# Delta-rule attention and a top-2 expert layer on one core: a new order of the first tile's loads and small vector work, and expert numbers of the first two expert tiles read once

## Chip, cores, metric

One core of one Trainium2 chip. The time is device microseconds of one launch; the kernel before took 901.56 us, the median of 3 runs (900.86 to 904.77). All start times below are microseconds from the start of the profiled span.

## What is computed

The reference, cut to what matters (x is 8 x 512 x 256 in fp32; 4 heads with keys of 128 and values of 64; 8 experts with a hidden width of 1024):

```python
x = x + attn(layernorm(x))          # delta rule
#  q, k, v, g = x@Wq, x@Wk, x@Wv, x@Wg ; beta = sigmoid(x@Wb)
#  k = k * rsqrt(sum(k*k) + 1e-12) ; q = q * DK**-0.5
#  per token: S += k (beta (v - k.S))^T ; o = q.S
#  o = o * rsqrt(mean(o*o) + eps) * norm_w * silu(g) ; return o @ Wo
x = x + ffn(layernorm(x))
#  probs = softmax(x @ router.T) ; the best 2 of 8 experts per token
#  out = sum over the 2 of prob * (gelu(x @ w1[e].T) @ w2[e].T)
```

## The kernel before, in words

Everything is written by hand, one instruction stream per engine, with a named semaphore for each hand-over. An engine executes its stream in order, so the order of the Python calls is the schedule.

**Attention.** The 4096 tokens are T = 32 tiles of 128. Each engine has a loop over i in which it calls stages of several tiles at once (`gram(i - 2)`, `k_proj(i - 1)` and so on): a software pipeline that is fixed in the program text. Tile n goes through: `ln1_stats` (DVE, line 1716: BN_STATS, BN_AGGR, add eps), `ln1_scale` (POOL, line 622: a power -0.5 at line 620, then a product at line 630), `ln1` (ACT, xn), `xnT_make` (PE transposes, line 1203), `xnT_evac` and `xnT_low` (fp16 high part by ACT, low part by DVE, line 1732), `k_proj`, `beta_proj`, `q_proj` (PE), `k_square` and `beta_exp` (ACT), `k_norm` (DVE, lines 1761 and 1763: the argument karg), `kscale_` (POOL: karg to the power -0.5 in line 620), `k_prime` (DVE, line 1772: k' = k times kscale), `k_transposes` (PE, line 1262), `kT_evac` (ACT) and `kT_low` (DVE, line 1747), `gram` (PE), `masked_l` (DVE, line 1792, nL), and then the inversion of a triangular matrix in 7 levels, the state update and the output. All products run as three fp16 products of high and low parts, so each weight is split too: `weight_hi(n)` on ACT, then `weight_lo(n)` on DVE (line 1906; n = 1 is wq, 2 is wvg, 3 is wo) and `wk_lo` (line 2082).

**Before the loops** stand the prologues. SP issues the loads (x tile 0, the small constants of `fc`, the identity `ident`, wb, wq, ...). POOL's prologue is `ln1_scale(0)`, one line on rowA that waits for `fc`, and `ln1_scale(1)`; its loop then begins with `kscale_(0)`. The change doesn't touch POOL's stream.

**Experts.** After the attention, tokens are gathered by expert into tiles of 256 tokens. `up(i, q, ms)` makes the hidden layer of expert tile 4i+q, 8 groups m of 6 matmuls with 256 columns; `down(i, q, ms)` makes the output from 8 groups m of 4 matmuls (columns 512, 256, 512, 256). Which expert a tile has is a number in SBUF (`tile_table`) that PE's sequencer reads into a register (`expert_of`, line 1558: TENSOR_LOAD), since the number is an address of the weights. `up` and `down` read it anew on each call. Between the parts of the first expert tiles stand the last steps of attention tile T-1: `xn2T_make`, `logits_make`, `rank` and others. ACT applies gelu (`hidden`), DVE makes the low part (`hidden_lo`, line 2266) and then the routing of the last group (`best_logit` to `expert_masks`, which writes `both`), and PE's `rank` (8 small matmuls) needs `both`.

```python
def parts_of(i, q):
    ...
    return [(expert_of(i, q), slice(0, PE_TOK))]

def ln1_scale(n):
    ...
    done(pool, s_mv, n)
```

Of the kernel before, what the change touches and what calls it, by code (L numbers as in the profile page):

```python
# [4 lines left out]
P = 128  # L5
# [3 lines left out]
T = B * N // P  # L9
# [3 lines left out]
KH = HID // P  # L13
EPS = 1e-5
PE_TOK = 2 * P
# [56 lines left out]
def build(nc, x, wq, wk, wvg, wb, wo, norm_w, router, w1, w2, eye, fconst, iconst, out):  # L72
# [3 lines left out]
    with ctx:  # L76
# [16 lines left out]
        wq_s, wk_s = wqk[:, 0, :, :, :], wqk[:, 1, :, :, :]  # L93
# [366 lines left out]
        def _(sp):  # L460
# [40 lines left out]
            load_x(0)  # L501
            sp.dma_start(fc[:, 3 * P:FCONST], fconst[:, 3 * P:FCONST]).then_inc(s_fc, 16)
            sp.dma_start(ident, fconst[:, 0:P]).then_inc(s_ident, 16)
# [288 lines left out]
        def _(act):  # L792
# [173 lines left out]
            def weight_hi(n, dst, src, scale=A_SCALE):  # L966
                act.wait_ge(s_wload[n], 16)
                evac(dst, src, scale).then_inc(s_wsh, 1)
# [30 lines left out]
            weight_hi(2, wvg_s[:, 0, :, :], wvg_in)  # L999
            k_square(0)  # L1000
            beta_exp(0)
            q_evac(0)
# [144 lines left out]
            xn2T_evac(T - 1)  # L1147
            logits_copy(T - 1)
            hidden(0, 0, range(3, 4))
# [19 lines left out]
        def _(pe):  # L1169
# [405 lines left out]
            def up(i, q, ms=range(KH)):  # L1575
                owners = parts_of(i, q)
# [47 lines left out]
            up(0, 0, range(0, 2))  # L1624
# [4 lines left out]
            up(0, 0, range(2, 4))  # L1629
# [3 lines left out]
            up(0, 0, range(4, 6))  # L1633
            wo_make(T - 1)
            done(pe, s_z, T - 1)
            up(0, 0, range(6, 8))
            up(0, 1, range(0, 2))
            xn2T_make(T - 1)
            up(0, 1, range(2, 4))
            logits_make(T - 1)  # L1640

            up(0, 1, range(4, 6))
            xT_make(0, 2)
            up(0, 1, range(6, 8))
            done(pe, s_lg, T - 1)
            rank(T - 1, p_rank_last, p_tot_last)
# [3 lines left out]
            down(0, 0)  # L1650
# [49 lines left out]
        def _(dve):  # L1700
# [371 lines left out]
            def next_stats(n):  # L2072
                if n > 1:
                    ln1_stats(n)
# [14 lines left out]
            dve.scalar_tensor_tensor(wb_s[:, 1, :, :], wb_in[:, :, :], A_SCALE, wb_s[:, 0, :, :], ALU.mult, ALU.subtract).then_inc(s_wbl, 1)  # L2089
            ln1_stats(1)  # L2090
            dve.wait_ge(s_fc, 16)
# [4 lines left out]
            weight_lo(1, wq_s, wq_in).then_inc(s_wsl, 1)  # L2096
            weight_lo(2, wvg_s, wvg_in).then_inc(s_wsl, 1)
            k_norm(0)
# [10 lines left out]
            q_low(0)  # L2109
            k_prime(0)  # L2110
            dve.wait_ge(s_normw, 1)
            weight_lo(3, wo_s, wo_in, normw_s[:, 0:1]).then_inc(s_wsl, 1)
# [89 lines left out]
            for i in range(T + 3):  # L2202
# [40 lines left out]
                kT_low(i - 3)  # L2243
# [121 lines left out]
            hidden_lo(0, 0, range(0, 3))  # L2365
# [13 lines left out]
            hidden_lo(0, 0, range(3, 4))  # L2379
# [99 lines left out]
```

## Time and profile before

| what | value |
|---|---|
| median of 3 runs | 901.56 us (900.86 to 904.77) |
| the profiled execution | 903.63 us, of which the span is 901.8 us |
| PE busy | 846.8 us (94%) |
| DVE busy | 627.8 us (70%) |
| ACT busy | 596.9 us (66%) |
| POOL busy | 441.0 us (49%) |
| mean granted TensorE clock | 0.984 of full |

The table is read from the top: the span is what the engines did, the 1.8 us more are around it. A busy share is an average over stages (the first 60 us, the attention loop to about 490 us, the first expert tiles, the expert loop) and doesn't tell which engine ends a stage; the rows further below do.

### The profile page before, as it was taken

Reading aid. Unit: us, or ns where it says so; the run is one execution under the profiler, and the core shown is the slowest. Engines: PE = TensorE matmul, PEld = TensorE weight load, DVE = VectorE, ACT = ScalarE, POOL = GpSimd, SP = SyncE. Lnnn points to the kernel's source line nnn. Section 1 sums busy time; section 2 is a strip of 40 time slices with the busy share of each in tenths; the row PEclk is TensorE's granted clock in tenths of the full one; section 3 lists DMA queues with packets and bytes.
Section 4 is the critical chain, followed back from the end, with each engine's and each line's share of the span. In section 5 each row is a group of like instructions: output and inputs, shape, how many; then the busy total and the mean of one; then the engine's idle time right before and its main releaser. Section 6 shows DMA issues by size and latency. Waiting matters only on the chain.

```text
span 901.8 us, 29514 instructions
## 1 busy us (share of the span) xinstructions
PE 846.8 (94%) x9870; PEld 667.9 (74%) x9871; DVE 627.8 (70%) x1833; ACT 596.9 (66%) x1646; POOL 441.0 (49%) x431
## 2 busy tenths in 40 slices
PE   4799999999999999999988999999999999999995
PEld 2578877788877888778876677777777777777772
DVE  6588897898988989889885675554455555555552
ACT  4588888888888888888775855444455444545550
POOL 3255454767767676776646553322233233333333
PEclk9999999999999999999996999999999999999998
DMA  6022221323233332322332163322233323333323
GB/s 228 2 78 71 86 84 61 106 80 103 84 101 98 88 106 80 103 84 90 91 113 82 57 148 50 58 45 42 37 62 60 48 47 47 47 47 47 48 37 35
DMA packets 50652, 67.14 MB, mean 74 GB/s; under 512 B 6464, under 2 KB 35008, under 8 KB 50528
## 3 DMA queue, kind: packets, MB, share of 16 engines
q1 hardware_dynamic: 36640, 46.46, 18.2%
q0 software_dynamic: 13344, 17.97, 11.7%
q8 instruction: 79, 1.29, 0.6%
q10 hardware_dynamic: 544, 1.05, 0.3%
q14 instruction: 45, 0.37, 0.1%
HBM read 41.84 MB, written 23.61 MB: 73 GB/s over the span
## 4 chain that ended last, share of the span: by engine, by line
PE 61%; POOL 6%; issue 5%; ACT 4%; DMA 4%; DVE 3%; SPq 0%; DVEq 0%; POOLq 0%; ACTq 0%
PE ps L1171 57%; DMA wst<-w 3%; PE ps L1551 2%; POOL kscale L620 1%; ACT inverse_levels L794 1%; PE ps L1262 1%; POOL w_lo L669 1%; POOL Ll L683 1%; DVE inverse_levels L1833 1%; PE ps L1428 1%; POOL ors L620 1%; POOL w_s L669 1%; POOL routed_rows L698 1%; DVE nL L1792 1%; PE ps L1203 1%
## 5 line engine op out<-in xcount | busy, mean ns | idle before, releaser
L794 ACT ACTIVATE inverse_levels<-ps 128x512 f16<-128x512 f32 (+1 forms) x324 | 162.6, 518 | 152.9 <-PE ps L1551 124.3
L774 POOL DMA_INDIRECT out<-inverse_levels,yidx x71 | 119.5, 1683 | 248.6 <-DVE inverse_levels L2303 181.6
L1171 PE MATMUL ps<-inverse_levels,w_hi 128*128 128x256 f16 (+1 forms) x1376 | 192.2, 255 | 1.1 <-issue 1.1
L2266 DVE SCALAR_TENSOR_TENSOR KpAT<-kq_wvg,inverse_levels 128x512 f16<-128x512 f32 (+1 forms) x144 | 98.4, 687 | 102.9 <-ACT inverse_levels L794 102.8
L1171 PE MATMUL ps<-inverse_levels,w_lo 128*128 128x256 f16 (+1 forms) x688 | 163.9, 254 | 0.0
L1171 PE MATMUL ps<-w_s,inverse_levels 128*128 x426 | 141.8, 379 | 6.5 <-issue 3.3
L1171 PEld LDWEIGHTS ps<-inverse_levels,w_hi 128*128 x1376 | 125.3, 98 | 14.5 <-issue 2.2
L1068 ACT ACTIVATE kq_wvg<-ps 128x512 f32<-128x512 f32 (+1 forms) x144 | 84.9, 590 | 54.7 <-PE ps L1171 51.0
L1171 PE MATMUL ps<-w_s,KpAT 128*128 x426 | 116.1, 273 | 0.0
L1833 DVE CAST_PREDICATED inverse_levels<-mask_s,ps 128x256 f16<-128x256 int8 x192 | 82.3, 429 | 16.0 <-PE ps L1171 10.0
L794 ACT ACTIVATE inverse_levels<-kq_wvg 128x512 f16<-128x512 f32 (+1 forms) x144 | 89.8, 624 | 4.5
L620 POOL TENSOR_TENSOR kscale<-karg,half_neg 128x8 f32<-128x8 f32 x32 | 52.7, 1647 | 73.2 <-DVE karg L1763 73.2
L1171 PEld LDWEIGHTS ps<-w_s,inverse_levels 128*128 128x128 f16 x426 | 41.6, 98 | 54.0 <-issue 10.1
L1171 PE MATMUL ps<-wqk,inverse_levels 128*128 128x512 f16 (+1 forms) x263 | 78.2, 385 | 1.1 <-ACT inverse_levels L794 1.0
L2299 DVE TENSOR_SCALAR inverse_levels<-ps,gate 128x256 f32<-128x256 f32 x69 | 30.3, 480 | 69.8 <-PE ps L1171 69.7
L1171 PE MATMUL ps<-inverse_levels 128*128 128x64 f16 x1408 | 69.0, 194 | 10.1 <-DVE inverse_levels L1833 9.8
L698 POOL DMA_INDIRECT routed_rows<-rowA,slot x64 | 67.4, 1053 | 18.2 <-issue 12.5
L1171 PEld LDWEIGHTS ps<-inverse_levels 128*128 128x128 f16 x1408 | 56.1, 99 | 23.6 <-DVE inverse_levels L1833 14.7
L1171 PE MATMUL ps<-kq_wvg,inverse_levels 128*128 128x512 f16 (+1 forms) x263 | 73.0, 385 | 0.0
L1171 PE MATMUL ps<-inverse_levels,Lh 128*128 128x64 f16 x896 | 64.3, 195 | 9.1 <-ACT inverse_levels L794 5.3
L1171 PEld LDWEIGHTS ps<-inverse_levels,w_lo 128*128 x688 | 67.5, 98 | 5.2
L1171 PEld LDWEIGHTS ps<-inverse_levels,Lh 128*128 128x128 f16 x896 | 47.1, 100 | 21.7 <-ACT inverse_levels L794 12.2
(241 smaller groups left out, 1921.3 us busy)
## 6 DMA issues: line engine op xcount, KB each, us to landing
wst<-w SPq DMA_DIRECT2D x58, 256.0 KB
inverse_levels<-eye SPq DMA_DIRECT2D x35, 256.0 KB, 2.7
x_s<-x SPq DMA_DIRECT2D x32, 128.0 KB, 2.7
out<-x_s SPq DMA_DIRECT2D x32, 128.0 KB, 1.7
x_s<-routed_rows SPq DMA_DIRECT2D x7, 260.0 KB
Lh<-routed_rows SPq DMA_DIRECT2D x7, 260.0 KB, 2.8
Vp<-routed_rows SPq DMA_DIRECT2D x7, 260.0 KB
rowA<-routed_rows SPq DMA_DIRECT2D x7, 260.0 KB, 3.0
```

Source lines behind the costliest of these rows:

```text
L620: return pool.tensor_tensor(dst, src, half_neg[:, 0:n], ALU.pow)
L669: pool.tensor_tensor(lo, src, hi, ALU.subtract).then_inc(s_wlo, 1)
L683: pool.tensor_tensor(Ll[:, :, :], nL[:, :, :], Lh[:, n % RING, :, :], ALU.subtract).then_inc(s_Ll, 1)
L698: pool.indirect_dma_start(out=routed, out_offset=bass.IndirectOffsetOnAxis(ap=slot[:, g % 2, k, c:c + 1], axis=0), in_=rowA[:, g % RG * C ...
L774: pool.indirect_dma_start(out=out, out_offset=bass.IndirectOffsetOnAxis(ap=yidx[:, q, a:a + 1], axis=0), in_=yrow[:, q % 2, a, :], in_offs ...
L794: return act.activation(dst, src, ACT.Copy, scale=scale)
L1068: act.activation(gelu, p_h[m].rearrange("p (m n) -> p m n", m=2)[:, :, 0:n], ACT.Gelu, scale=1.0 / W_SCALE).then_inc(s_gelu, 1)
L1171: return pe.matmul(dst, lhsT, rhs, start=start, stop=stop, **kw)
L1551: last = pe.transpose(p_gT[:, k, a * P:(a + 1) * P], xg[q % 4][:, a, k * P:(k + 1) * P], ident)
L1833: dve.copy_predicated(even(Y[:, lev - 1, :, :], lev), level_mask(lev, 0, H), packed(p_y[q], lev)).then_inc(s_ys[q], 1)
L2266: dve.scalar_tensor_tensor(hlo[:, q % 2, two, 0:n], hf[:, m, :].rearrange("p (m n) -> p m n", m=2)[:, :, 0:n], H_SCALE, hhi[:, q % 2, two, ...
L2299: step(dve.tensor_scalar(yrow[:, par, a, :], p_yo[a][:, 0, :], gate[:, par, a:a + 1], None, ALU.mult))
```

## The change

It edits four places. (1) SP: the identity is loaded before the small constants. (2) ACT: `weight_hi(2)` (wvg) moves behind `k_square(0)` and `beta_exp(0)`. (3) DVE's prologue has a new order: `weight_lo(1)` and `k_norm(0)` come before `ln1_stats(1)`; `q_low(0)` and `k_prime(0)` come before the seven instructions that prepare constants; `kT_low(0)` moves from the loop into the prologue, and `ln1_stats(2)` too. (4) The first expert tiles: the expert numbers of tiles 0 and 1 are read once and kept in registers; `xn2T_make(T-1)` and `logits_make(T-1)` come two m-groups later among the parts of `up(0, 1)`; `rank(T-1)` moves from ahead of `down(0, 0)` to behind its first six groups. On ACT and DVE the fourth part of the hidden layer of tile 0 moves ahead of the logits and the routing.

```diff
@@ SP
             load_x(0)
+            sp.dma_start(ident, fconst[:, 0:P]).then_inc(s_ident, 16)
             sp.dma_start(fc[:, 3 * P:FCONST], fconst[:, 3 * P:FCONST]).then_inc(s_fc, 16)
-            sp.dma_start(ident, fconst[:, 0:P]).then_inc(s_ident, 16)
@@ ACT
             weight_hi(1, wq_s[:, 0, :, :], wq_in)
-            weight_hi(2, wvg_s[:, 0, :, :], wvg_in)
             k_square(0)
             beta_exp(0)
+            weight_hi(2, wvg_s[:, 0, :, :], wvg_in)
...
             xn2T_evac(T - 1)
+            hidden(0, 0, range(3, 4))
             logits_copy(T - 1)
-            hidden(0, 0, range(3, 4))
@@ PE
-            def up(i, q, ms=range(KH)):
-                owners = parts_of(i, q)
+            def up(i, q, ms=range(KH), owners=None):
+                owners = owners or parts_of(i, q)
...
-            up(0, 0, range(0, 2))
+            tiles = [[(expert_of(0, q), slice(0, PE_TOK))] for q in range(2)]
+            up(0, 0, range(0, 2), tiles[0])
...
-            up(0, 0, range(6, 8))
-            up(0, 1, range(0, 2))
+            up(0, 0, range(6, 8), tiles[0])
+            up(0, 1, range(0, 4), tiles[1])
             xn2T_make(T - 1)
-            up(0, 1, range(2, 4))
+            up(0, 1, range(4, 6), tiles[1])
             logits_make(T - 1)
-
-            up(0, 1, range(4, 6))
             xT_make(0, 2)
-            up(0, 1, range(6, 8))
-            done(pe, s_lg, T - 1)
-            rank(T - 1, p_rank_last, p_tot_last)
+            up(0, 1, range(6, 8), tiles[1])
             pe.wait_ge(s_pos, G - 1)
             pe.wait_ge(s_whi, 2 * T)
             pe.wait_ge(s_wlo, 2 * T)
-            down(0, 0)
+            down(0, 0, range(0, 6), [tiles[0][0][0]])
+            done(pe, s_lg, T - 1)
+            rank(T - 1, p_rank_last, p_tot_last)
+            down(0, 0, range(6, 8), [tiles[0][0][0]])
@@ DVE
             def next_stats(n):
-                if n > 1:
+                if n > 2:
                     ln1_stats(n)
...
+            weight_lo(1, wq_s, wq_in).then_inc(s_wsl, 1)
+            dve.wait_ge(s_fc, 16)
+            k_norm(0)
             ln1_stats(1)
-            dve.wait_ge(s_fc, 16)
+            weight_lo(2, wvg_s, wvg_in).then_inc(s_wsl, 1)
             dve.wait_ge(s_ident, 16)
             dve.wait_ge(s_tri, 16)
             dve.wait_ge(s_normw_in, 16)
             dve.tensor_scalar(normw_s[:, :], normw_s[:, :], A_SCALE, None, ALU.mult).then_inc(s_normw, 1)
-            weight_lo(1, wq_s, wq_in).then_inc(s_wsl, 1)
-            weight_lo(2, wvg_s, wvg_in).then_inc(s_wsl, 1)
-            k_norm(0)
+            q_low(0)
+            k_prime(0)
             step(dve.tensor_copy(posI[:, :], ident))
...
             dve.sem_inc(s_init, 1)
-            q_low(0)
-            k_prime(0)
             dve.wait_ge(s_normw, 1)
+            kT_low(0)
+            ln1_stats(2)
             weight_lo(3, wo_s, wo_in, normw_s[:, 0:1]).then_inc(s_wsl, 1)
...
-                kT_low(i - 3)
+                if i > 3:
+                    kT_low(i - 3)
...
-            hidden_lo(0, 0, range(0, 3))
+            hidden_lo(0, 0)
...
             expert_masks(T - 1)
-            hidden_lo(0, 0, range(3, 4))
             xT_lo(0, 2)
```

**DVE's prologue.** The stream of DVE from its second `wk_lo` on; first before (wqk with 1024 elements is `weight_lo(1)`, kq_wvg with 1024 is `weight_lo(2)`, the rows karg are `k_norm(0)`, st and mv are `ln1_stats`):

```order
L2089 SCALAR_TENSOR_TENSOR wb_s<-wb_in,wb_s 128x8
L1720 BN_STATS st<-x_s 128x6
L1723 BN_AGGR mv<-st 128x2
L1724 TENSOR_SCALAR mv<-mv 128x1
L2095 TENSOR_SCALAR normw_s<-normw_s 128x1
L1906 SCALAR_TENSOR_TENSOR wqk<-w_s,wqk 128x1024
L1906 SCALAR_TENSOR_TENSOR kq_wvg<-w_s,kq_wvg 128x1024
L1761 SCALAR_TENSOR_TENSOR karg<-eb,fc 128x4
L1763 SCALAR_TENSOR_TENSOR karg<-ks,karg 128x4
```

and now:

```order
L2089 SCALAR_TENSOR_TENSOR wb_s<-wb_in,wb_s 128x8
L1906 SCALAR_TENSOR_TENSOR wqk<-w_s,wqk 128x1024
L1761 SCALAR_TENSOR_TENSOR karg<-eb,fc 128x4
L1763 SCALAR_TENSOR_TENSOR karg<-ks,karg 128x4
L1720 BN_STATS st<-x_s 128x6
L1723 BN_AGGR mv<-st 128x2
L1724 TENSOR_SCALAR mv<-mv 128x1
L1906 SCALAR_TENSOR_TENSOR kq_wvg<-w_s,kq_wvg 128x1024
```

`ln1_stats(1)` now stands behind both rows of karg, and directly ahead of `weight_lo(2)`.

**POOL's prologue**, the same in both kernels:

```order
L709 TENSOR_SCALAR rowA<-rowA,fc 128x2
L620 TENSOR_TENSOR rs<-mv,half_neg 128x1
L630 TENSOR_SCALAR rs<-mv,rs 128x1
L620 TENSOR_TENSOR kscale<-karg,half_neg 128x8
```

The pair rs is `ln1_scale(1)`, which takes mv; `kscale_(0)`, which takes karg, comes behind it.

**PE at the end of `up(0, 1)`**, first before (w_hi_7 and w_lo_7 are its last group, both and before16 or ones16 are `rank`, w2_s is `down`):

```order
L1171 MATMUL ps4<-inverse_levels,w1_lo_1_7 128x256
L1171 MATMUL ps7<-both,before16 128x32
L1171 MATMUL ps7<-both,ones16 128x24
L1171 MATMUL ps7<-both,ones16 128x16
L1171 MATMUL ps7<-both,ones16 128x8 x5
L1558 TENSOR_LOAD tile_table
L1558 ISA x2
L1171 ISA
L1171 MATMUL ps56<-w2_s,inverse_levels 128x512
```

and now (up to the first matmul of `down`, then from its sixth group to the seventh):

```order
L1171 MATMUL ps4<-inverse_levels,w1_lo_1_7 128x256
L1171 ISA
L1171 MATMUL ps56<-w2_s,inverse_levels 128x512
...
L1171 MATMUL ps56<-w2_s,KpAT 128x256
L1171 MATMUL ps7<-both,before16 128x32
L1171 MATMUL ps7<-both,ones16 128x24
L1171 MATMUL ps7<-both,ones16 128x16
L1171 MATMUL ps7<-both,ones16 128x8 x5
L1171 REGISTER_ALU
L1171 MATMUL ps56<-wqk,inverse_levels 128x512
```

The TENSOR_LOAD ahead of `down` is gone, as are six others between the parts of `up`; two stand together ahead of `up(0, 0)`.

## Rows read from the trace of the kernel before

**Rows 1.** Busy time by stretch, the expert loop: PE, PEld, DVE, ACT, POOL, clock, DMA

```profile
520.00:560.00 40.00, 40.00 (x306) 29.92 (x305) 25.44 (x73) 19.00 (x32) 18.17 (x14) 1.00 0.48 104
```

**Rows 2.** Timeline of the first tile: start, duration, engine, line, [idle before <-releaser]

```profile
5.49 0.60 ACT L802 ACTIVATE inverse_levels<-x_s,rs 128x256 f32<-128x256 f32 x1 [2.49 <-POOL rs L630]
7.12 0.69 PE L1203 MATMUL ps<-fc,inverse_levels 128*128 128x128 f32 x2 [7.12 <-DMA fc<-fconst]
8.26 0.42 DVE L1732 TENSOR_TENSOR inverse_levels<-ps,inverse_levels 128x256 f16<-128x256 f32 x1 [0.92 <-ACT inverse_levels L794]
```

**Rows 3.** The load of the small constants: its issue, and KB and us to landing

```profile
1.18 0.43 SPq L502 DMA_DIRECT2D fc<-fconst  x1
...
fc<-fconst SPq DMA_DIRECT2D x1, 81.5 KB, 3.8
```

**Rows 4.** Timeline of POOL, 10 to 18 us

```profile
10.37 1.65 POOL L620 TENSOR_TENSOR rs<-mv,half_neg 128x1 f32<-128x1 f32 x1 [4.51 <-DVE mv L1724]
12.12 0.75 POOL L630 TENSOR_SCALAR rs<-mv,rs 128x1 f32<-128x1 f32 x1
13.22 1.70 POOL L620 TENSOR_TENSOR kscale<-karg,half_neg 128x8 f32<-128x8 f32 x1 [0.34 <-DVE karg L1763]
17.12 0.54 POOL L620 TENSOR_TENSOR rs<-mv,half_neg 128x1 f32<-128x1 f32 x1 [2.20 <-DVE mv L1724]
```

**Rows 5.** Timeline of DVE and ACT, 9 to 20 us

```profile
9.69 1.04 ACT L794 ACTIVATE kq_wvg<-w_s 128x1024 f16<-128x1024 f32 x1
10.39 1.22 DVE L1906 SCALAR_TENSOR_TENSOR wqk<-w_s,wqk 128x1024 f16<-128x1024 f32 x1
13.05 0.22 DVE L2099 CAST posI<-fc 128x128 f16<-128x128 f32 x1
13.88 0.22 DVE L2106 TENSOR_SCALAR fc<-fc 128x128 f32<-128x128 f32 x1
14.95 0.69 DVE L1772 TENSOR_TENSOR KpAT<-ps,kscale 128x512 f32<-128x512 f32 x1
15.56 0.74 DVE L1906 SCALAR_TENSOR_TENSOR wo_s<-w_s,normw_s,wo_s 128x512 f16<-128x512 f32 x1
16.45 0.60 ACT L794 ACTIVATE kq_wvg<-ps 128x512 f16<-128x512 f32 x1 [1.28 <-PE ps L1262]
17.70 0.68 DVE L1747 TENSOR_TENSOR kq_wvg<-ps,kq_wvg 128x512 f16<-128x512 f32 x1
19.99 0.69 DVE L1792 TENSOR_TENSOR nL<-ps,fc 128x512 f32<-128x512 f32 x1 [0.59 <-PE ps L1171]
```

**Rows 6.** PE's sequencer reading the expert number, 494 to 510 us: ns min/median/max

```profile
L1558 PEldq TENSOR_LOAD <-tile_table x7: 297/302/548, 495.6 to 508.4; - x7
```

**Rows 7.** Timeline of PE, 498 to 510 us, the parts of the first expert tiles

```profile
498.06 0.81 PE L1171 MATMUL ps<-wo_s,inverse_levels 128*128 128x256 f16 x6
499.04 0.39 PE L1171 MATMUL ps<-inverse_levels,w_hi 128*128 128x256 f16 x2 [0.17 <-issue]
...
500.71 0.39 PE L1171 MATMUL ps<-inverse_levels,w_hi 128*128 128x256 f16 x2 [0.19 <-issue]
...
502.52 0.41 PE L1460 MATMUL ps<-fc,rowA 128*128 128x128 f32 x2 [0.33 <-ACT rowA L814]
503.29 0.39 PE L1171 MATMUL ps<-inverse_levels,w_hi 128*128 128x256 f16 x2 [0.36 <-issue]
...
504.61 0.51 PE L1171 MATMUL ps<-router_s,inverse_levels 128*128 128x8 f32 x4
505.31 0.39 PE L1171 MATMUL ps<-inverse_levels,w_hi 128*128 128x256 f16 x2 [0.20 <-issue]
...
508.38 0.18 PE L1171 MATMUL ps<-both,before 128*128 128x32 f16 x1
...
509.50 0.39 PE L1171 MATMUL ps<-w_s,inverse_levels 128*128 x1 [0.78 <-ACT inverse_levels L794]
```

**Rows 8.** Busy time by stretch, 30 to 32 us (columns as in rows 1)

```profile
30.00:32.00 2.00, 2.00 (x10) 0.79 (x8) 1.02 (x2) 0.90 (x2) 0.20 (x1) 0.50 0.00 0
```

More of the change, by code:

```diff
@@ L1628, in _ @@
             done(pe, s_kp, T - 1)
-            up(0, 0, range(2, 4))
+            up(0, 0, range(2, 4), tiles[0])
             xT_make(0, 1)
@@ L1632, in _ @@
             done(pe, s_on, T - 1)
-            up(0, 0, range(4, 6))
+            up(0, 0, range(4, 6), tiles[0])
             wo_make(T - 1)
             done(pe, s_z, T - 1)
-            up(0, 0, range(6, 8))
-            up(0, 1, range(0, 2))
+            up(0, 0, range(6, 8), tiles[0])
+            up(0, 1, range(0, 4), tiles[1])
             xn2T_make(T - 1)
-            up(0, 1, range(2, 4))
+            up(0, 1, range(4, 6), tiles[1])
             logits_make(T - 1)
-            up(0, 1, range(4, 6))
             xT_make(0, 2)
-            up(0, 1, range(6, 8))
-            done(pe, s_lg, T - 1)
-            rank(T - 1, p_rank_last, p_tot_last)
+            up(0, 1, range(6, 8), tiles[1])
             pe.wait_ge(s_pos, G - 1)
```

## Prediction, on record before the changed kernel ran

> **What bounds the kernel now.** I read the busy times by stretch first, then the timelines of the two places that the change touches. In the expert loop PE is busy 40.00 of 40.00 us at full clock while DVE and ACT have time over [rows 1]; what comes earlier or later there moves the end by as much. So a shift at 509.50 us, where the first `down` begins, should reach the end whole. The first 20 us are the opposite: tile 0 alone goes from engine to engine, each waits for the one before it, and PE's in-order loop hangs on the result (nL at 19.99 us [rows 5], from which the whole inversion of tile 0 starts). Nothing in the loop runs on a clock of its own, so a shift of nL(0) also reaches the end whole, unless a slack in the ramp that I don't see takes it up.
>
> So the change has two sums, one for nL(0) and one for the first `down`.
>
> **First tile, part by part.**
>
> *Identity first.* PE's first transposes start at 7.12, released by the load of the identity, while xn is ready at 5.49 + 0.60 = 6.09 [rows 2]. The constants that are now behind it were issued at 1.18 and took 3.8 to land [rows 3], so the identity in that place lands near 4.98 and xn becomes the wait: transposes near 6.2. The low part xnT (8.26) moves by the same 0.9, and the k projection behind it. Bound: 0 (if another load or weight holds the projection) to 0.9; I take 0.87, since k's first weight half isn't late. The swapped constants land about 2 us later; their only early reader, POOL's line on rowA, has nothing behind it before 10.37.
>
> *karg earlier.* With wvg's split out of its way on both engines, karg follows the projection: kscale, released by karg, started at 13.22 [rows 4], and could start at 12.35.
>
> *But POOL's order was not changed.* Ahead of kscale(0) POOL has ln1_scale(1), which waits for mv of tile 1, and these statistics now come behind karg on DVE. karg ends near 13.13 - 0.87 = 12.26. One set of statistics takes 0.74: wo's low part and two sets fill 15.56 to 17.70 (2.14), of which wo is 0.66. With the first wait mv is there at 13.1. POOL's power on one column takes 0.54 when DVE is quiet (17.12), but it took 1.65 at 10.37 [rows 4], and 10.39 is where DVE began its 1.22 us split of 1024 elements [rows 5]: the power ended 0.41 after that. In the new order the very same instruction, wvg's low part, again follows mv directly (ACT's part of it, 1.04 us, is ready by 12.9: eb ends near 11.85). So the power runs from 13.15 to 14.34 + 0.41 = 14.75, its product takes 0.4 with its wait, and kscale runs 15.15 to 16.8. k' starts at 16.85, against 14.95 now: **1.9 later**, not 0.9 earlier. Without the contention it would be 15.85.
>
> The Trainium skill, GPSIMD Engine Reference, Specifications, says that GpSimd's SBUF interfaces are shared with VectorE and contend with DVE instructions that have two SBUF inputs, which this split is. By that rule the sum for this step is the 1.9 just given, by the quiet row alone 0.9; the 1.65 against 0.54 agrees with the rule.
>
> *From k' to nL.* Before, the seven constant instructions (13.05 to 13.88 + 0.22 = 14.10, 1.05 us) lay in the wait for kscale at no cost. Now they stand behind k', and cost 1.05: 16.85 + 0.61 + 1.05 = 18.5. The transposed k passes PE and ACT meanwhile: k' ended at 15.64 and ACT's copy at 17.05, so 1.41; now 17.54 + 1.41 + 0.05 = 19.0 starts kT_low. It gains, since the two statistics and wo's split no longer stand ahead of it, but they stand behind it and ahead of nL all the same. Between 15.56 and 19.99 DVE has 3.22 of such work besides kT_low (4.43 less 0.61 for kT_low and 0.59 idle). So nL(0) is at 19.0 + 0.61 + 3.22 = 22.8, against 19.99: **2.8 later** (1.8 if POOL isn't held).
>
> *Clock.* PE idles from about 12.9 to 15.9 (the transposes of tile 1 now wait for POOL too) and almost to 17.7. Before, the granted clock fell to 0.50 at 30 to 32 [rows 8] after a stretch with such holes. At that level, 1.2 instead of 2.4 GHz, the v and g projection and the gram of tile 0 take some 2.5 us more, of which 1.4 would lie under DVE's work: nL at 23.9. I take half of the 1.1, 0.5. The start costs 2.8 + 0.5 = **3.3**; bounds 1.8 (POOL not held, no clock) and 3.9 (the whole 1.1), and a gain of 0.9 as a rival below.
>
> **First expert tiles.** Seven reads of the expert number lie between 494 and 510, 0.30 to 0.55 us each [rows 6], with register work behind. What they cost is the distance from start to start over the plain pace. Twelve matmuls of 256 columns take 1.31 where nothing disturbs them (503.29 to 504.61), so 0.109 each. From 498.06 on [rows 7]: wo's six matmuls 0.98 for 0.65, over by 0.33; 499.04 to 500.71 is 1.67 for 1.31, over by 0.36; to 502.52, 1.81 for 1.31, 0.50 (a wait for ACT's rowA, which the new place of xn2T_make lets pass behind two more groups); to 503.29, 0.77 for 0.22, 0.55; 504.61 to 505.31, 0.70 for some 0.40, 0.30; 508.38 to 509.50, 1.12 for 0.33, 0.79. Sum 2.83. The read ahead of `up(0, 0, 4:6)` gives nothing: wo at 498.06 waits for oT's low part. The read ahead of `up(0, 0)` becomes two, some 0.6 longer, of which part is hidden behind the slow matmuls in front: 0.25. Gelu of the third pair is ready just when `up(0, 1, 4:6)` now wants its bank: 0.15. Net **2.4 earlier**, bounds 1.0 and 2.8.
>
> *rank.* It costs its 0.33 in either place. Left where it was it would take the gain away: PE would be there 2 us earlier than now, but `both`, at the end of a DVE chain that starts with the logits, would be ready 0.6 later than now, because the fourth low part of the hidden layer (0.7) is now ahead of it. Behind six groups of `down` (6 x 0.65 = 3.9 us) it waits for nothing. The groups of `down` up to the sixth need hidden parts 1 to 3 and all late weights, which are there. The positions and the scatters that follow rank on DVE and POOL are then held, as now, by DVE's hidden parts ahead of them; next late would be ACT, with 1.15 us per hidden part against 1.31 of PE.
>
> **Sum.** 3.3 - 2.4 = 0.9 later. The profiled execution (903.63, span 901.8) would come to 904.5; it stood 2.1 over the median 901.56, so by the median **902.5 us**. About 0.5% (4.5 us) is what a measurement can tell from no change, and the runs before alone spread by 3.9.
>
> **Rivals.**
> - *The start gains* (0.15): kscale isn't held, by a slack in POOL or DVE that I overlook, and the 0.9 of the identity reaches nL. Against it speaks POOL's fixed order. Then -0.9 - 2.4 = -3.3: 898.3.
> - *The reads are replaced by a wait* (0.20): ACT's gelu chain, 1.15 us per part and with a table load before it, sets PE's pace from 500 on, and only 1.0 of the 2.4 is left: +2.3, 903.9. For it: two waits on gelu lie within 0.2 us of PE's new times. Against: before the change PE waited there for none.
> - *The clock decides* (0.05), the case on the slow side: the holes at 13 to 17 us bring more stretches at 0.50, in the ramp and again around the first expert tiles, where the gain is then paid back. The start would cost 2.8 + 1.1 + 1.7 (half of one more stretch of the length at 29 to 32.4), and of 2.4 remain 0.5: about +5.1, 906.7. It decides from the point where the start's loss exceeds the experts' gain by 4.5.
> - *The change does only half* (0.05): the middle gains and the start is neutral, the ramp absorbing 2.8: -2.4, 899.2.
>
> **How the numbers follow.** My forecast has 0.55. The range takes in the first, second and fourth rival: 898.5 to 905.3 (3.9 at the start with only 1.0 gained gives +2.9, 904.5, and the spread of a median of three adds near 1). Faster by over 0.5% needs -4.5, more than either part can give: 0.04. Slower by over 0.5%: 0.05. The rest, 0.91, is within.
>
> **What would show it.** In the new profile: transposes at 6.2; POOL's rs of tile 1 near 13.1 with 1.6 us, and kscale behind it near 15.1; k' near 16.9 and nL near 22.8. Then the distance from the start of `up(0, 0)` to the first `down`: 17.7 us before, near 15 now, and at the next expert tile's transposes 2.4 less. The forecast is wrong if kscale starts before 14, if nL(0) is not later, or if the loop from 60 us on doesn't carry the shift.

## The result, and the profile after

The changed kernel took **905.94 us** (median of 22 runs), the kernel before 901.94 us on the same chip (22 runs); the ratio is **1.0036, 95% interval 1.0022 to 1.0051**, so 3.2 us slower (2.0 to 4.6); the two medians are 4.0 apart. The forecast was 0.9 slower, within 0.5% (4.5 us) of no change. The difference of 3.2 lies below these 4.5 us, and inside the forecast's range if that is read as a difference (3.1 faster to 3.7 slower, 898.5 and 905.3 against 901.56). The absolute 905.94 is 0.6 above the range's upper end.

| what | before | changed |
|---|---|---|
| profiled execution, us | 903.63 | 905.29 |
| its span | 901.8 | 903.5 |
| PE busy | 846.8 | 849.5 (94%) |
| mean granted TensorE clock | 0.984 | 0.976 |
| nL of tile 0 starts (DVE) | 19.99 | 22.82 |
| nL of tile 1 starts | 34.48 | 38.61 |
| first `up` group of tile 0 starts (PE) | 491.76 | 495.37 |
| first `down` starts | 509.50 | 510.82 |
| transposes of expert tile 3 start | 514.71 | 516.22 |

The first tile, in the timeline of the changed kernel (start, duration, engine, line, in brackets the idle time before and its releaser), PE, then DVE, then POOL; the rows of before are [rows 2, 4, 5]:

```profile
6.00 0.66 PE L1203 MATMUL ps<-fc,inverse_levels 128*128 128x128 f32 x2 [6.00 <-ACT inverse_levels L802]
15.50 0.66 PE L1203 MATMUL ps<-fc,inverse_levels 128*128 128x128 f32 x2 [3.37 <-ACT inverse_levels L802]
17.22 1.09 PE L1262 MATMUL ps<-fc,KpAT 128*128 128x128 f32 x4 [1.05 <-DVE KpAT L1772]
18.09 2.77 PE L1171 MATMUL ps<-kq_wvg,inverse_levels 128*128 128x512 f16 x6
```

```profile
11.91 0.16 DVE L1763 SCALAR_TENSOR_TENSOR karg<-ks,karg 128x4 f32<-128x4 f32 x1
12.66 0.15 DVE L1724 TENSOR_SCALAR mv<-mv 128x1 f32<-128x1 f32 x1
12.73 1.22 DVE L1906 SCALAR_TENSOR_TENSOR kq_wvg<-w_s,kq_wvg 128x1024 f16<-128x1024 f32 x1
16.38 0.69 DVE L1772 TENSOR_TENSOR KpAT<-ps,kscale 128x512 f32<-128x512 f32 x1 [1.77 <-POOL kscale L620]
19.04 0.69 DVE L1747 TENSOR_TENSOR kq_wvg<-ps,kq_wvg 128x512 f16<-128x512 f32 x1 [1.00 <-ACT kq_wvg L794]
22.82 0.68 DVE L1792 TENSOR_TENSOR nL<-ps,fc 128x512 f32<-128x512 f32 x1
```

```profile
12.90 1.46 POOL L620 TENSOR_TENSOR rs<-mv,half_neg 128x1 f32<-128x1 f32 x1 [5.62 <-DVE mv L1724]
14.46 0.27 POOL L630 TENSOR_SCALAR rs<-mv,rs 128x1 f32<-128x1 f32 x1
14.68 1.66 POOL L620 TENSOR_TENSOR kscale<-karg,half_neg 128x8 f32<-128x8 f32 x1
```

The reader sees the forecast's chain row by row. karg is complete at 12.07, 1.1 us earlier than before, and still kscale starts at 14.68 instead of 13.22, because POOL's stream has rs(1) first, and rs(1) starts only at 12.90 and takes 1.46. From there everything is late: the transposes of tile 1 (PE idle for 3.37 us ahead of them), k', and nL(0). nL(0) has no idle time before it, so DVE's own work ends last there, as the sum said. The v and g projection took 2.77 us in place of 1.46; the busy times by stretch show why (columns as in rows 1, the clock is the third number from the right):

```profile
12.00:14.00 2.00, 0.13 (x3) 0.00 (x0) 1.93 (x7) 1.03 (x2) 1.10 (x1) 1.00 1.05 376
14.00:16.00 2.00, 0.50 (x2) 0.29 (x2) 0.61 (x2) 1.21 (x2) 1.90 (x3) 0.53 1.06 377
16.00:18.00 2.00, 0.95 (x5) 0.81 (x5) 1.59 (x8) 0.00 (x0) 0.34 (x1) 0.50 0.27 99
18.00:20.00 2.00, 2.00 (x7) 0.79 (x6) 0.99 (x3) 0.60 (x1) 0.00 (x0) 0.50 0.00 0
```

PE had worked 0.13 of 2.00 us when the granted clock fell to its lower level, 1.2 GHz, and it stayed there until 21.0 (6.8 us at half clock, from 14.2). A second such stretch, 6.8 us long, lies at 31.2 to 38.0 us, where before one of 3.4 lay at 29.3 to 32.7 [rows 8]. nL(1) is 4.1 later although nL(0) is only 2.8 later; the longer stretch accounts for this in part or whole.

Around the first expert tiles, PE of the changed kernel (the rows of before are [rows 7]):

```profile
494.35 0.64 PE L1460 MATMUL ps<-fc,rowA 128*128 128x128 f32 x2
495.37 0.60 PE L1171 MATMUL ps<-inverse_levels,w_hi 128*128 128x256 f16 x2 [0.38 <-issue]
...
502.43 0.81 PE L1171 MATMUL ps<-wo_s,inverse_levels 128*128 128x256 f16 x6 [0.31 <-DVE inverse_levels L1739]
...
507.11 0.40 PE L1460 MATMUL ps<-fc,rowA 128*128 128x128 f32 x2
...
508.67 0.51 PE L1171 MATMUL ps<-router_s,inverse_levels 128*128 128x8 f32 x4
...
510.82 0.38 PE L1171 MATMUL ps<-w_s,inverse_levels 128*128 x1
...
514.72 0.18 PE L1171 MATMUL ps<-both,before 128*128 128x32 f16 x1
...
516.22 0.60 PE L1551 MATMUL ps<-fc,rowA 128*128 128x128 f32 x4
```

and the three rows of before that go with them:

```profile
491.34 0.64 PE L1460 MATMUL ps<-fc,rowA 128*128 128x128 f32 x2
491.76 0.63 PE L1171 MATMUL ps<-inverse_levels,w_hi 128*128 128x256 f16 x2
...
514.71 0.60 PE L1551 MATMUL ps<-fc,rowA 128*128 128x128 f32 x4
```

Before, there are nine reads of the expert number for these two tiles (at 490.4, at 493.1 and seven from 495.6 to 508.4). Two are left, both ahead of the first `up` (493.4 and 494.2), so the edit takes away the one ahead of `down` and seven between the parts of `up`, not six. All the waits named "issue" between 498 and 510 are gone, and so is the wait on rowA ahead of xn2T. From wo to the first `down` PE needs 8.39 us, before 11.44. Since `rank` now lies behind it, the fair distance is from wo to the transposes of expert tile 3, which has the same work in both kernels: 13.79 against 16.65, **2.86 less**. From the first `up` to wo it is 7.06 against 6.30, 0.76 more, although reads are gone there too: the clock is at its lower level for the first 3.4 us of this stretch, where before it was so for 1.7, and half of the difference, 0.9, is what that costs. So 2.10 are gained from the first `up` on. Ahead of it the second read shows: from the start of the transposes of xn2T(T-2) (494.35, before 491.34) to the first `up` it is 1.02 against 0.42, 0.60 more. Of the shift of 3.01 at 494.35 there is 1.51 left at the transposes of tile 3. In the loop behind it PE is busy 40.00 of 40.00 us as in [rows 1], and the end of the span is 1.7 later.

The 2.86 are the steady part of this account. From wo to the transposes of tile 3 all eight other kernels with the whole edit and `rank` at its new place lie between 13.78 and 13.95, and the two others with the old order and the old reads (e2, e7) at 16.65 and 16.71. The stretch from the first `up` to wo, in contrast, varies from trace to trace (5.42 to 7.64 among the changed ones, 5.97 to 6.30 among the old ones) with the moment at which the stretch at half clock ends.

### The profile page after: what moved, and what is told of

It reads as the page before. It is cut to its first block, busy times and chain, and to the rows that moved or that the text cites. A ratio compares the mean times of both kernels' runs of the same rounds, so it can differ in the third digit from the quotient of the medians.

```text
span 903.5 us, 29493 instructions
## 1 busy us (share of the span) xinstructions
PE 849.5 (94%) x9870; PEld 669.6 (74%) x9871; DVE 626.9 (69%) x1833; ACT 596.3 (66%) x1646; POOL 441.2 (49%) x431
## 3 DMA queue, kind: packets, MB, share of 16 engines
q10 hardware_dynamic: 544, 1.05, 0.3%
## 4 chain that ended last, share of the span: by engine, by line
PE 63%; POOL 6%; issue 4%; DVE 3%; DMA 3%; ACT 3%; DVEq 0%; POOLq 0%; ACTq 0%
PE ps L1171 59%; DMA wst<-w 3%; PE ps L1551 2%; POOL kscale L620 1%; PE ps L1262 1%; ACT inverse_levels L794 1%; POOL Ll L683 1%; POOL w_s L669 1%; POOL w_lo L669 1%; PE ps L1428 1%; DVE inverse_levels L1833 1%; POOL ors L620 1%; PE ps L1203 1%; POOL routed_rows L698 1%; DVE nL L1792 1%
```

## The experiments

All comparisons are with the kernel before, run on the same chip in the same rounds. The experiments ran on two other chips, on which the kernel before took 911.87 and 909.99 us, and again 911.64 on the first of them.

**Each part alone.** The expert edits alone (with the edits on ACT and DVE that belong to them), and the start alone:

```diff
e1: the kernel before, with only
+            tiles = [[(expert_of(0, q), slice(0, PE_TOK))] for q in range(2)]
...
+            down(0, 0, range(0, 6), [tiles[0][0][0]])
+            done(pe, s_lg, T - 1)
+            rank(T - 1, p_rank_last, p_tot_last)
+            down(0, 0, range(6, 8), [tiles[0][0][0]])
e2: the kernel before, with only the edits to SP, to ACT's prologue and to DVE's prologue
```

> The kernel before with the fourth edit alone (the first expert tiles on PE, ACT and DVE). Theory (the change is a loss in the first tile and a gain of about 2.1 us at the expert tiles, each carried to the end): nL(0) stays at 20.0 us, the first up to the first down takes about 15.0 to 15.5 us instead of 17.7, the next expert tile's transposes come 2.1 to 2.4 earlier, time 899.7 us. Rival (the gain at the expert tiles is paid back later or never reaches the end): time 901.9 us, transposes earlier but the end not.

> The kernel before with the first three edits alone (loads, ACT and DVE of the first tile). Theory: nL(0) at 22.8 us as in the changed kernel, nL(1) about 4 us later than before, time 905.5 to 907 us, so above the changed kernel by the gain of the expert part. Rival (the loss is not of the start but of the clock around the expert tiles): time near 902 us.

Measured: e1 0.9977 (0.9953 to 1.0001), 2.1 us faster; from the first `up` to the transposes of tile 3 20.72 us, against 22.95. e2 1.0034 (1.0016 to 1.0053), 3.1 us slower; nL(0) at 23.48. So the two parts have the signs of the forecast, and their sizes are 2.1 (2.4 forecast) and 3.1 (3.3 forecast); the interval of e1 just includes no gain. Their sum is 1.0 slower. nL(0) of e2 is later than the 22.8 that was expected, and it has a wait for PE that the changed kernel doesn't have:

```profile
23.48 0.69 DVE L1792 TENSOR_TENSOR nL<-ps,fc 128x512 f32<-128x512 f32 x1 [0.50 <-PE ps L1171]
```

The stretch at half clock lies 2.3 us later there, at 16.5 to 23.3, and takes in PE's gram of tile 0 (2.72 us for 1.47 before). The whole was then run again on the third chip:

> The changed kernel itself, on the chip and in the rounds of the other variants, since chips differ by some 10 us and the parts are to be added up. If the two parts add (+3.1 for the first tile, -2.1 for the expert tiles) it comes to a ratio of 1.001; the comparison made first gave 1.0036. In the trace: nL(0) at 22.8 us, first up to first down 15.0 to 15.5 us.

Measured: 1.0030 (1.0013 to 1.0046), 2.7 us slower, with nL(0) at 22.97 and 20.14 us from the first `up` to the transposes of tile 3. The whole is thus 1.7 to 2.2 more than its parts. The three intervals are 0.15 to 0.24% to either side, together some 3 us, so this difference isn't clear of noise. What the clock says of it comes below.

**POOL's order.** Only the order of POOL is changed here, and then only DVE's:

```diff
e3: the changed kernel, POOL
+            kscale_(0)
             ln1_scale(1)
e4: the changed kernel, DVE
+            ln1_stats(1)
             weight_lo(1, wq_s, wq_in).then_inc(s_wsl, 1)
             dve.wait_ge(s_fc, 16)
             k_norm(0)
-            ln1_stats(1)
```

> The changed kernel with one line of POOL moved: kscale of tile 0 ahead of the statistics' scale of tile 1. Theory (POOL's fixed order holds kscale behind tile 1's mv): kscale starts near 12.1 instead of 14.7 us, k' near 14.5 (then held by DVE's own wvg split and q low part), nL(0) near 20.5 instead of 22.8, the half clock of 14 to 21 us shortened or gone, time 901 to 902.5 us. Rival (DVE's order is the loss: constants and statistics behind k'): k' earlier but nL(0) at 22 or later, time 905 us.

> The changed kernel with the statistics of tile 1 ahead of wq's low part on DVE again, where DVE was idle for 0.82 us. Theory: mv of tile 1 near 9.2, POOL's power on it is still stretched (by wq's split now) but done by 11.2, kscale near 12.1, k' near 14.5, nL(0) near 20.4, time 901 to 902.5 us, the same as with POOL's line moved. Rival (DVE's order behind k' is the loss): nL(0) at 22 or later, time 905 us.

POOL's rows of e3, then of e4:

```profile
12.06 1.67 POOL L620 TENSOR_TENSOR kscale<-karg,half_neg 128x8 f32<-128x8 f32 x1 [4.87 <-DVE karg L1765]
13.69 0.56 POOL L620 TENSOR_TENSOR rs<-mv,half_neg 128x1 f32<-128x1 f32 x1
```

```profile
9.75 1.46 POOL L620 TENSOR_TENSOR rs<-mv,half_neg 128x1 f32<-128x1 f32 x1 [1.98 <-DVE mv L1724]
12.64 1.66 POOL L620 TENSOR_TENSOR kscale<-karg,half_neg 128x8 f32<-128x8 f32 x1 [1.06 <-DVE karg L1763]
```

With kscale first it starts at 12.06, right behind karg, and k' at 14.43, 1.95 earlier than in the changed kernel; with the statistics back in front it starts at 12.64 and k' at 14.87. So the statement on POOL's order holds: it is what held kscale. But only 1.0 and 1.8 us of it reached nL(0) (21.83 and 21.01), and both expectations of it, 20.5 and 20.4, were missed. In e3 PE still stood idle for 3.02 us until 15.39, its transposes of k took 1.06 at half clock, kT_low came at 17.64 only, the constants stood behind k', and nL(0) waited 0.32 us for PE. e4 prices the last point: its k' starts at 14.87, as before the change (14.95), and its nL(0) is 1.0 later than before, the size of the 1.05 us of constants that are now behind k'. Times against the kernel before: 1.0013 (0.9994 to 1.0032) and 1.0007 (0.998 to 1.0035), so neither is told apart from no change.

**The contention.** What stretches rs(1)? In e9 the split of wvg is moved behind k':

```diff
e9: the changed kernel, DVE
             ln1_stats(1)
-            weight_lo(2, wvg_s, wvg_in).then_inc(s_wsl, 1)
...
             k_prime(0)
+            weight_lo(2, wvg_s, wvg_in).then_inc(s_wsl, 1)
```

> The changed kernel, with DVE's split of wvg (1.22 us) moved from directly behind the statistics of tile 1 to behind k'. If an instruction with two SBUF inputs on DVE is what stretches POOL's power, rs(1) takes 0.5 to 0.6 us in place of 1.46, kscale starts near 13.8 in place of 14.68 and k' near 15.4 in place of 16.38. If the stretch has another cause (the first use of the power after a pause, the cold start), rs(1) takes 1.4 to 1.6 again and kscale starts as before. nL(0) stays within 0.5 of 22.8 either way, since the 1.2 us now stand behind k'; the time against the kernel before 1.000 to 1.006.

```profile
12.98 0.56 POOL L620 TENSOR_TENSOR rs<-mv,half_neg 128x1 f32<-128x1 f32 x1 [5.61 <-DVE mv L1724]
13.64 0.26 POOL L630 TENSOR_SCALAR rs<-mv,rs 128x1 f32<-128x1 f32 x1
13.86 1.66 POOL L620 TENSOR_TENSOR kscale<-karg,half_neg 128x8 f32<-128x8 f32 x1
```

The same power on the same data, again after a pause of 5.6 us, takes 0.56 in place of 1.46. The split is the cause, the pause isn't. kscale starts 0.8 earlier and k' at 15.55. nL(0) is hardly earlier, at 22.72: the split now stands ahead of it on DVE, and its last wait is for PE, which has half clock from 15.7 to 22.5:

```profile
22.72 0.69 DVE L1792 TENSOR_TENSOR nL<-ps,fc 128x512 f32<-128x512 f32 x1 [0.30 <-PE ps L1171]
```

The time is 1.0025 (0.9993 to 1.0056).

**The hole on PE.** This kernel adds work that computes nothing: 14 matmuls into a bank that nobody reads before the gram overwrites it.

```diff
e11: the changed kernel, PE
+                for _ in range(10 if i == 1 else 0):
+                    mm(PS[6][:, :], xnT[:, 0, 0, :], wq_s[:, 0, 0, :])
                 xnT_make(i)
+                for _ in range(4 if i == 1 else 0):
+                    mm(PS[6][:, :], xnT[:, 0, 0, :], wq_s[:, 0, 0, :])
```

> The changed kernel with 14 matmuls of 512 columns added on PE, whose results nobody reads: 10 where PE waits for the transposes of tile 1 (12.1 to 15.5) and 4 between these and the transposes of k (16.2 to 17.2). If the holes are what brings the half clock, the clock stays full, the v and g projection takes about 1.4 us in place of 2.77, nL(0) stays at 22.8 plus or minus 0.3 (DVE's own work ends last there) and nL(1) comes back by 1 to 1.5 us against the changed kernel on the same chip. If the clock falls whatever PE does, all these stay as in the changed kernel. The time against the kernel before: 1.000 to 1.003 by the first, 1.003 to 1.004 by the second.

PE's timeline and its busy times by stretch in e11:

```profile
13.10 2.66 PE L1171 MATMUL ps<-wqk,inverse_levels 128*128 128x512 f16 x10
15.68 0.41 PE L1203 MATMUL ps<-fc,inverse_levels 128*128 128x128 f32 x2
15.93 1.03 PE L1171 MATMUL ps<-wqk,inverse_levels 128*128 128x512 f16 x4
17.39 0.63 PE L1262 MATMUL ps<-fc,KpAT 128*128 128x128 f32 x4 [0.43 <-DVE KpAT L1776]
17.86 1.46 PE L1171 MATMUL ps<-kq_wvg,inverse_levels 128*128 128x512 f16 x6
```

```profile
14.00:16.00 2.00, 2.00 (x12) 0.93 (x10) 0.78 (x3) 1.06 (x2) 1.90 (x3) 1.00 1.08 383
16.00:18.00 2.00, 1.56 (x10) 0.81 (x9) 1.41 (x8) 0.15 (x1) 0.52 (x1) 1.00 0.30 110
18.00:20.00 2.00, 1.77 (x12) 0.82 (x10) 1.42 (x5) 1.19 (x3) 0.00 (x0) 1.00 0.00 0
```

The clock stays full through the stretch, the v and g projection takes 1.46, and nL(0) is at 22.54, 0.3 earlier, although k' came 0.17 later (16.55). From k' to nL(0) it is 5.99 us, in the changed kernel 6.44 and in e2, with its later stretch at half clock, 7.04. So half clock costs nL(0) 0.45 in the changed kernel, by way of the transposes of k, and 1.05 in e2, where nL(0) also waits for the gram; the rest of it lies under DVE's own work. nL(1) comes at 36.21 (the changed kernel: 38.61 in its first trace, 36.81 in that of e5). Yet the time was not better: 1.0034 (1.0008 to 1.0059). In this trace other stretches at half clock follow, of 3.4 us each, at 24, 112 and 129 us, and what had been won is gone by tile 9 (nL at 155.73, changed kernel 151.82). Ahead of the one at 112 the attention loop waits for a weight of the experts that is still being loaded, ACT's row being

```profile
110.97 0.63 ACT L794 ACTIVATE w_s<-wst 128x512 f16<-128x512 f32 x1 [1.58 <-DMA wst<-w]
```

Such waits of ACT for the weight `w_s` are in every trace of this case, 3.3 to 8.9 us in all between 40 and 480 us. So filling the hole kept the clock up, in this one trace; all seven other traces with the new order on DVE have the projection at 2.58 to 2.77. The hole isn't the only way to it: of the six traces with DVE's old order five have 1.46 and one, e10, has 2.75. That the removal of the hole lowers the total was expected (1.000 to 1.003) and isn't seen; the interval still allows the upper part of it.

**The clock over all runs.** Each run has its mean granted clock. This record is incomplete, as the first tile of e8 (below) shows:

```profile
17.73 2.77 PE L1171 MATMUL ps<-kq_wvg,inverse_levels 128*128 128x512 f16 x6
```

```profile
18.00:20.00 2.00, 2.00 (x6) 0.74 (x5) 1.26 (x4) 0.57 (x1) 0.00 (x0) 1.00 0.00 0
```

The duration is that of half clock, the record says full. The first six matmuls of k's projection take 2.72 in every trace, again with 1.00 on record, and in e8 the slow pace lasts until 22.9. So the record leaves the first stretch of a run out, and a run whose clock rises late has too high a mean. Within sets of runs of one kernel on one chip (255 runs: 13 sets of the changed kernel and the experiments, three of the kernel before on the two other chips), a clock lower by 0.01 goes with a time longer by 4.4 us (standard error 0.3). Against the kernel before on the same chip the mean clock was lower by 0.0049 in e5, 0.0013 in e2, 0.0036 in e3, 0.0033 in e4, 0.0053 in e9, 0.0045 in e8 and 0.0040 in e11, all kernels with the new start (each difference has a standard error of 0.001 to 0.0015); it was 0.0001 lower in e1 and in e7 (below), and higher by 0.0012 and 0.0017 in e6 and e12, which have the expert edits and a start near the old one (below); e10, with the old start, has 0.0023 less and is the exception. For e5, 0.0049 times 437 (the 4.4 us per 0.01) is 2.1 us. That is about what the whole costs beyond the forecast's 0.9, but it is a comparison and no experiment. e2 has the same start, 3.1 us of loss and only 0.0013 less clock; e11, which keeps the clock up where the change lets it fall, has the low mean all the same. Where the half clock lies matters too: the two profiled executions differ by 0.008 in mean clock, and half of this difference is a stretch of 6.8 us at 471 to 478 us, behind which the shift is 3.0 after 2.8 ahead of it.

**Rank and the registers.** Two kernels take the expert edit apart:

```diff
e8: the changed kernel, PE
+            done(pe, s_lg, T - 1)
+            rank(T - 1, p_rank_last, p_tot_last)
             pe.wait_ge(s_pos, G - 1)
...
-            down(0, 0, range(0, 6), [tiles[0][0][0]])
-            done(pe, s_lg, T - 1)
-            rank(T - 1, p_rank_last, p_tot_last)
-            down(0, 0, range(6, 8), [tiles[0][0][0]])
+            down(0, 0, range(KH), [tiles[0][0][0]])
e10: the kernel before, its order kept, with only
+            tiles = [[(expert_of(0, q), slice(0, PE_TOK))] for q in range(2)]
and these passed to each up(0, 0, ...), up(0, 1, ...) and down(0, 0)
```

> The changed kernel with rank of the last group ahead of the first down again, the rest as changed. Theory: PE arrives at rank 2 us before its input is ready and waits, so the first down starts some 1.8 to 2.2 us later than in the changed kernel and the gain of the expert edits is gone; time 2 us over the changed kernel. Rival (the place of rank costs nothing, since what follows is held by ACT or DVE): the transposes of expert tile 3 as in the changed kernel.

> The kernel before, with the expert numbers of tiles 0 and 1 kept in registers, and every order left as it was. If the seven reads are the whole loss, the distance from the first up to the transposes of expert tile 3 falls from 22.95 by 2.4 or so. My theory: PE comes to the last ranks earlier but there waits for both, which DVE writes no earlier than before, so only what lies behind it (the read ahead of the first down, about 0.8) is gained: 22.2 to 22.6. nL(0) as in the kernel before (near 20).

In e8, PE and DVE:

```profile
508.66 0.27 PE L1171 MATMUL ps<-inverse_levels,w_lo 128*128 128x256 f16 x1
510.76 0.18 PE L1171 MATMUL ps<-both,before 128*128 128x32 f16 x1 [1.82 <-issue]
...
511.70 0.63 PE L1171 MATMUL ps<-w_s,inverse_levels 128*128 x1
```

```profile
510.46 0.19 DVE L1918 SCALAR_TENSOR_TENSOR both<-chosen 128x32 f16<-128x32 f32 x1
```

The page calls the idle time "issue", but it is the wait for `both`, which ends at 510.65; and right behind it the clock falls, so that the large matmuls of `down` take 0.63 in place of 0.38 (511.7 to 515). Together they cost 3.7 us from wo to the transposes of tile 3 (17.54 against 13.79); the time is 1.0058 (1.0034 to 1.0082), where the whole change had 1.0030 on that chip.

In e10 the reads are gone and the order is the old one, PE again:

```profile
507.87 0.41 PE L1460 MATMUL ps<-fc,rowA 128*128 128x128 f32 x2 [1.03 <-ACT rowA L814]
```

PE comes earlier to xn2T and waits there 1.03 us for ACT's rowA (before 0.33), and to `rank` within 0.15 us of the end of `both`. From wo to the transposes of tile 3 it takes 15.24: 1.4 of the 2.86 come from the registers alone, the other half from the two new places, of xn2T and of rank. My expected 22.2 to 22.6 from the first `up` was missed (22.94): the clock was at its lower level for the first 4.7 us of that stretch, against 1.7 before, which by half of the difference explains some 1.5 us. The time, 1.0015 (0.9989 to 1.0041), shows no gain.

**A better start.** What of the start is worth keeping? The identity alone, then two versions of the whole:

```diff
e7: the kernel before, SP
+            sp.dma_start(ident, fconst[:, 0:P]).then_inc(s_ident, 16)
             sp.dma_start(fc[:, 3 * P:FCONST], fconst[:, 3 * P:FCONST]).then_inc(s_fc, 16)
-            sp.dma_start(ident, fconst[:, 0:P]).then_inc(s_ident, 16)
e12: e7, with the expert edits, and the second number read later:
-            tiles = [[(expert_of(0, q), slice(0, PE_TOK))] for q in range(2)]
+            tiles = [[(expert_of(0, 0), slice(0, PE_TOK))]]
             up(0, 0, range(0, 2), tiles[0])
+            tiles.append([(expert_of(0, 1), slice(0, PE_TOK))])
e6: e12, with kT_low(0) behind weight_lo(3) and ln1_stats(2) in DVE's prologue
```

> The kernel before with the two loads swapped and nothing else. Theory: transposes of tile 0 near 6.0 instead of 7.1, k projection 1 us earlier, kscale near 12.1, nL(0) near 19.0 (1.0 earlier); ratio near 0.999. Rival (the small constants that land later hold POOL or DVE): nL(0) at 20.0 or later, ratio 1.000.

> A version from the findings: the kernel before with the identity first, kT's low part of tile 0 ahead of the third statistics, and the expert edits, with the second expert number read behind the first two groups instead of ahead of them. The other first-tile edits (ACT's and DVE's order) are left out, since POOL's wait and PE's hole come from them. Theory: kscale near 12.1, k' near 13.9, nL(0) near 18.4 (1.6 earlier than before), first up to first down 15.0 us; time 3.5 to 4.5 us under the kernel before, ratio 0.995 to 0.996. Rival (what is gained in the first tile is taken by the ramp's clock or waits): ratio 0.9975, the expert edits alone.

> The kernel before, with the two loads swapped (identity first) and the whole edit of the first expert tiles, the second expert number read one part later; nothing else of the start is changed. If the start's loss came from the new order on DVE, this keeps nL(0) at 19.0 to 19.8 and has a distance from the first up to the first down of 14.7 to 15.3: 0.995 to 0.998 of the kernel before.

Measured: e7 1.0006 (0.998 to 1.0032), with nL(0) at 18.95, 1.04 earlier than before and nothing of it visible in the time. e6 0.9965 (0.9946 to 0.9984), 3.2 us faster, with nL(0) at 19.79, so the expected 18.4 was missed: kscale started at 12.63 (12.1 expected), and on DVE k' stands behind `q_low(0)`, which waited 1.16 us for ACT's copy of q. **e12 0.9955 (0.9931 to 0.9979), 4.1 us faster than the kernel before**, with nL(0) at 19.49 and 13.95 us from wo to the transposes of tile 3. Against the changed kernel, by the two ratios on different chips, that is some 0.75%. How much of e12's gain is the identity's isn't shown: the expert edits alone (e1, 0.9977) have an interval that overlaps with it. The place of the second read does show: with one read ahead of the first `up` the distance from the transposes of xn2T(T-2) to it is 0.43 in e12 and e6, as in the kernel before (0.42), and with both reads there it is 0.89 to 1.08 in the eight traces in which this place has half clock.

## Why the prediction was right or wrong

*Where the time is bound.* Right, as far as these traces show it. In the pair of the two profiled executions the shift at tile 0 was carried whole: nL of the last tile is 2.75 later, nL(0) 2.83. But the distance from the first nL to the last varies from 441.3 to 448.5 us over the fourteen traces, so that one pair which agrees to 0.1 is luck in part. That the loss of the start reaches the end is shown by the times of e2 (3.1, at least 1.5). In between it was more (4.1 from tile 1 to tile 9) and was given back at tile 10, where the kernel before had a half-clock stretch (152 to 155 us) and the changed kernel had none.

*Identity first.* 6.2 forecast, 6.00 measured, released by xn. k's projection starts at 7.64 for 8.78.

*POOL's order and the contention.* Right, and shown by e3, e4 and e9. rs at 12.90 with 1.46 (13.15 and 1.6 forecast), kscale at 14.68 (15.15), k' at 16.38 (16.85): all 0.25 to 0.5 early, from a start 0.3 earlier and a product that took 0.27 without a wait of its own. The rule of the Trainium skill (GPSIMD Engine Reference, Specifications) on the shared SBUF interfaces agrees with this case's traces: the power took 1.46 beside the split and 0.56 without it (e9). k' was 1.4 later, for 1.9 by the sum.

*From k' to nL.* The 0.5 gained up to k' was lost again behind it: the transposes of k ran at half clock (1.09 for 0.63), ACT's copy came at 18.34, and kT_low started at 19.04 (19.0 forecast) after 1.00 us idle. From there DVE works without a gap to 22.82 (22.8). With its clock term the forecast was 22.8 + 0.5 = 23.3. So the hit at 22.8 is luck: the sum up to k' was 0.5 too late, and the half clock put 0.45 back.

*Clock.* At nL(0) the term is right in size: 0.5 taken, 0.45 measured against e11, and in e2 1.05 and in e8 1.09 (7.04 and 7.08 us from k' to nL(0)), the whole of the 1.1 that I had halved. **What the sum has no term for is the clock behind nL(0)**, and there the profiled pair has two losses: a stretch of half clock twice as long at 31 to 38 us (1.3 us at nL(1), which was given back at tile 10), and a stretch that reaches 1.7 us further into the first `up` (0.9 us). Over the runs of e5 the mean clock is 0.0049 lower, which goes with 2.1 us. The third rival described this case with +5.1 and a chance of 0.05; the measured +3.2 lies between my forecast and it (2.3 and 1.9 off). The number of the second rival, +2.3, is the nearest of all, and by luck, since the wait that it is built on didn't come. One profile doesn't show the size of the loss: the two profiled executions differ by 1.66, the medians by 4.0.

*The reads.* 2.83 less 0.4 forecast, 2.4; 1.50 measured in the profiled pair. From wo to the transposes of tile 3, 2.86 were gained; 0.76 of this was lost ahead of wo, to the clock, and 0.60 to the second read. For that I had 0.25, with cover from the slow matmuls ahead of it; the first read uses up this cover (0.43 with one read, 1.02 with two). The wait on gelu, 0.15, didn't come: from 502.5 to 513 the timeline names no wait of PE. That rival is refuted. e10 splits the gain: the reads alone are worth only half (1.4), since PE without them runs into rowA and then `both`. The sum of 2.83 needs the two new places, as the working said of each of them, though under a heading that speaks of the reads.

*rank.* Right: behind six groups of `down` it waits for nothing (514.72; `both` is written at 512.51 to 512.70), and left in front it takes the gain away (e8: 1.82 us of wait, and then the clock).

*Sum.* 0.9 forecast, 3.2 (2.0 to 4.6) measured. The parts alone give 1.0 (e1, e2). In the profiled pair the start cost 3.01 at the first expert tiles (3.3 forecast) and the edit there gained 1.50 (2.4 forecast), which leaves 1.51; the end of the span is 1.7 later. So the term that was mis-sized in the traces is the gain, by 0.9. The rest, from 1.7 to 3.2, is in no trace. It goes with a lower mean clock; whether the clock is its cause, or it is the chance of one comparison, stays open.

## What to carry to other kernels

When a producer is moved on one engine, read the consumer's whole in-order stream: kscale waited for statistics that it doesn't use. Cheap work that fills a wait isn't free at its new place; the seven constants cost their full 1.05 us there. And a wait on PE can cost twice its length where the clock falls behind it, as the 1.82 us in e8 did (3.7). Whether it falls differs from trace to trace, so a change of this size is to be judged by many runs and not by one pair of profiles.

## What the runs showed of the hardware

*Who is stretched by whom.* A POOL power on one column takes 0.54 to 0.56. Where it started within a DVE split with both inputs in SBUF (1.22 us), or 0.02 us ahead of one, it ended 0.39 to 0.43 us behind the split's end, whenever it had begun: 1.65 us in [rows 4], 1.46 in the changed kernel and in e4, 0.97 behind the shorter split of wo (0.74 us), and only 0.56 in e3, where it began 0.17 ahead of the split's end. The product on one column behind it, 0.26 to 0.27 elsewhere, took 0.75 where it began within the second split, and ended 0.13 behind its end [rows 4]. kscale, begun 0.4 to 0.6 us ahead of such a split (e3, e4), kept its 1.67. My reading is that the start of the instruction on POOL is what is held; no run tested it by itself. And in e9 kscale began during a DVE operation of 0.69 us with one input in PSUM, and also kept its 1.66.

*The record of the clock.* It doesn't cover the start of a run: matmuls at the pace of the lower level (2.72 us for six of 512 columns) stand beside a granted clock of 1.00 in every trace at 7 to 12 us, and in e8 such a pace does so up to 22.9 us.

*A stretch without instructions.* On the two other chips the kernels are some 8 to 10 us slower, the kernel before included, and the traces show one place for it. PE of e6, and two rows of its busy times by stretch:

```profile
525.39 0.38 PE L1171 MATMUL ps<-kq_wvg,inverse_levels 128*128 x1 [1.15 <-issue]
...
528.27 0.27 PE L1171 MATMUL ps<-kq_wvg,KpAT 128*128 x1 [1.06 <-issue]
529.66 0.56 PE L1551 MATMUL ps<-fc,x_s 128*128 128x128 f32 x2 [1.12 <-issue]
```

```profile
526.00:530.00 4.00, 1.26 (x5) 0.45 (x4) 0.45 (x1) 1.23 (x2) 3.28 (x3) 0.96 0.44 105
530.00:534.00 4.00, 3.12 (x16) 2.17 (x15) 3.20 (x12) 0.60 (x1) 0.89 (x1) 0.50 0.72 129
```

PE waits a microsecond at a time for nothing that the profile names, while ACT and DVE hardly work and SP issues eight DMAs for the padding rows. On the first chip the eight take 8.5 us together and PE is busy throughout; in e6 they take 13.2. The waits of PE add up to 5 us, and a stretch of half clock follows. What they wait for is open: that it is the loading of their own instructions is a guess, from the word "issue" and from its striking PE, ACT and DVE at once, and no run tested it.
